# Norms with the variance per token on partitions, and grouped attention with its projections in three rounded passes

## The reference

```python
x = x + tanh(g_xattn[0]) * L0_xattn(layernorm(x), ctx)   # 16 heads of 16, causal
x = x + tanh(g_ffn[0])   * L0_ffn(layernorm(x))          # 8 experts, top 1, and a shared one
x = x + tanh(g_xattn[1]) * L1_xattn(layernorm(x), ctx)   # 16 latent heads over all 1444 keys
x = x + tanh(g_ffn[1])   * L1_ffn(layernorm(x))

def L1_ffn(hidden):                       # hidden: output of layer norm "n3"
    resid = hidden
    h = rmsnorm(hidden, ln1_w)            # "r0"
    q, k, v = h @ Wq, h @ Wk, h @ Wv      # 32 query heads, 4 key heads, of 128
    x = resid + causal_attention(rope(q), rope(k), v) @ Wo
    h = rmsnorm(x, ln2_w)                 # "r1"
    return x + experts(h) + shared(h)     # 32 experts, top 8
```

## Time and profile before

| | us |
|---|---|
| median of three runs | 1648.06 |
| profiled execution, whole | 1648.92 |
| its span | 1647.1 |
| TensorE, matmuls busy | 1497.2 (91%) |
| VectorE busy | 904.1 (55%) |
| GpSimd busy | 725.7 (44%) |
| ScalarE busy | 600.1 (36%) |
| granted TensorE clock, mean of the span | 0.927 of full |

### The profile page before, as it was taken

One profiled execution on the slowest core, in us unless ns is written; L12 is line 12 of the kernel. 1 busy time (PEld: TensorE's weight loads), 2 busy tenths in 40 slices (PEclk: granted clock), 3 DMA queues, 4 the chain that ended last, 5 costly groups with the idle time before them and its releaser, 6 DMA issues. The chain is left out here.

```text
span 1647.1 us, 19563 instructions
## 1 busy us (share of the span) xinstructions
PE 1497.2 (91%) x6852; PEld 1047.1 (64%) x6852; DVE 904.1 (55%) x1530; ACT 600.1 (36%) x1034; POOL 725.7 (44%) x541
## 2 busy tenths in 40 slices
PE   6897999799978999999999998589999997699998
PEld 3685466444435675766766765246666664699997
DVE  2563111335666767767776643656666664354444
ACT  2332121123331344334343343355555553243333
POOL 1750202026554877787787564034444441133332
PEclk8797999579987999999999999799999999799999
DMA  8004111430001010010110000300000001244331
GB/s 291 1 1 140 49 46 36 142 110 22 23 3 65 24 55 26 30 55 1 55 55 1 18 2 9 122 1 26 24 28 26 1 1 39 85 128 123 117 118 48
DMA packets 60311, 88.53 MB, mean 54 GB/s; under 512 B 7556, under 2 KB 44612, under 8 KB 60230
## 3 DMA queue, kind: packets, MB, share of 16 engines
q1 hardware_dynamic: 59206, 85.82, 16.3%
q0 software_dynamic: 1024, 1.64, 0.4%
HBM read 81.92 MB, written 5.41 MB: 53 GB/s over the span
## 5 line engine op out<-in xcount | busy, mean ns | idle before, releaser
L670 POOL TENSOR_TENSOR xc<-xc,prob 121x800 f32<-121x800 f32 x112 | 230.2, 2055 | 69.2 <-ACT prob L906 60.9
L906 ACT ACTIVATE prob<-PS 121x800 f32<-121x800 f32 x192 | 159.1, 837 | 266.6 <-PE PS L1802 266.6
L1248 DVE TENSOR_REDUCE mx<-PS 128x1 f32<-128x482 f32 (+1 forms) x312 | 185.3, 643 | 72.8 <-PE PS L1782 72.0
L594 POOL TENSOR_TENSOR e_wl<-e_wf,e_wh 128x768 fp32r<-128x768 f32 x33 | 70.8, 2146 | 185.9 <-ACT e_wh L830 160.0
L1817 PE MATMUL PS<-prob,kvn 121*64 121x400 f32 (+1 forms) x768 | 142.1, 521 | 0.9 <-ACT prob L906 0.9
L1799 PE MATMUL PS<-qs,kth 128*121 128x400 f32 (+1 forms) x384 | 116.1, 385 | 21.2 <-DMA qm<-nml 18.3
L1781 PE MATMUL PS<-kth,qs 128*128 128x482 f32 (+1 forms) x312 | 125.8, 403 | 8.3 <-DVE kl L1241 5.8
L691 POOL TENSOR_TENSOR q<-q,qt 128x400 f32<-128x400 f32 x64 | 66.0, 1031 | 143.2 <-DVE qt L1366 143.2
L1782 PE MATMUL PS<-kl,qm 66*128 66x482 f32 (+1 forms) x312 | 121.4, 389 | 0.0
L1802 PE MATMUL PS<-qm,kl 66*121 66x400 f32 (+1 forms) x384 | 108.2, 365 | 0.0
L1799 PEld LDWEIGHTS PS<-qs,kth 128*121 128x121 f32 (+1 forms) x384 | 68.4, 196 | 60.7 <-DMA qm<-nml 20.9
(11 more groups left out here) (256 smaller groups left out, 3202.4 us busy)
## 6 DMA issues: line engine op xcount, KB each, us to landing
e_wb<-routing SPq DMA_DIRECT2D x32, 400.0 KB, 4.0
wgu<-in_L_ffn_gate_up_proj SPq DMA_DIRECT2D x8, 1024.0 KB, 14.2
krt<-in_ctx_T SPq DMA_DIRECT2D x8, 722.0 KB, 4.1
ksw<-in_ctx_Tswap SPq DMA_DIRECT2D x8, 722.0 KB, 5.7
wdn<-in_L_ffn_down_proj SPq DMA_DIRECT2D x8, 512.0 KB, 8.8
wq<-in_L_ffn_Wq SPq DMA_DIRECT2D x4, 1024.0 KB, 6.5
wo<-in_L_ffn_Wo SPq DMA_DIRECT2D x4, 1024.0 KB, 7.5
e_wf<-in_L_ffn_Wg SPq DMA_DIRECT2D x32, 128.0 KB, 2.2
```

The costliest lines, as they stand in the source:

```text
L670: pool.tensor_tensor(accp, accp, prob[:, n % RING], ALU.add).then_inc(xb["ap"], 1)
L906: act.activation(prob[0:k, n % RING], PS[0:k, 2 * (n % 2):2 * (n % 2) + 2, 0:GC], ACT.Exp).then_inc(xb["ex"], 1)
L1248: dve.tensor_reduce(mx3[:, m, g:g + 1], PS[:, 4 + k % 3, 0:SEG[g][1]], AX.X, ALU.max).then_inc(xb["free"], 1)
```

## The change

1. **Norms.** The squares are now the stationary operand and one column of `mean_w` the moving one, so that the variance comes out with tokens on partitions, as 100 x 8 numbers. Root and reciprocal work on these (`nsd`, `nrs`), and eight matmuls against the identity (`spread`) bring the result back onto 128 partitions in PSUM, where the products read it. A root of a constant (`warm`) stands first on ScalarE. r0 takes its variance from that of n3 (`nms`: variance times the squared inverse root) and follows in the same stage; n3's output goes straight to `R`.
2. **Latent attention.** `accp` gets a second buffer; the merge of the accumulators, the sums and the projection come later in a batch (steps 5, 6, 14 and 3, 4 after the twelfth), the four reciprocals of one half in one block at step 8, of the other at steps 20 to 23. `UNITS` ends one step earlier, and the turned maxima stand ahead of the values block of step 20.
3. **Grouped attention.** Query and output projections run in three passes over rounded parts. ScalarE rounds the weights in pieces of 256 columns, GpSimd subtracts for the low parts, VectorE splits the inputs and each unit's result (`low_values2`). Weights are single buffered, queries lie in a ring of ten, outputs start at step 9 (`BACK`).
4. **End.** The residual is added ahead of the experts of block 1, in the routing stage, so that the last chain has one instruction a piece in place of two.

```diff
-        UNITS = (0, 0, 0, 0, 2, 4, 6, 8, 11, 14, 16, 18, 21, 24, 26, 29, 30, 32, 34, 36, 39, 39, 39, 39, 39)
+        UNITS = (0, 0, 0, 0, 2, 4, 6, 8, 11, 14, 16, 18, 21, 24, 27, 30, 31, 33, 36, 39, 39, 39, 39, 39, 39)
-        U2, LEAD = 2 * B * G2, 6
+        U2, LEAD, BACK = 2 * B * G2, 6, 9
...
+            def low_query_weights(m):
+                v = slice(m % HG * P, (m % HG + 1) * P)
+                pool.wait_ge(fs["wqh"], XQ + m + 1)
+                pool.tensor_tensor(wql[:, :, v], wq2[:, :, v], wqh[:, :, v].bitcast(fp32), ALU.subtract).then_inc(fs["wql"], 1)
...
+                act.activation(wqh[:, :, v], wq2[:, :, v], ACT.Copy).then_inc(fs["wqh"], 1)
...
+                if query_split(s) is not None:
+                    high_query_weights(query_split(s))
+                if output_split(s) is not None:
+                    high_output_weights(output_split(s))
...
+            def low_values2(v):
+                x, k, b = unit2(v)
+                y = 2 * x + k
+                dve.wait_ge(at["pve"], U0 + v + 1)
+                dve.tensor_tensor(o2l[:, y % 3, :, b % HB, :], PS[:, 3, 0:4 * S].rearrange("p (h s) -> p h s", s=S),
+                                  o2h[:, y % 3, :, b % HB, :].bitcast(fp32), ALU.subtract).then_inc(fs["ol"], 1)
...
                 pe.wait_ge(at["pte"], U0 + v + 1)
                 if v >= 1:
-                    pe.wait_ge(at["pve"], U0 + v)
+                    pe.wait_ge(fs["ol"], XQ + v)
...
-                    last_ = mm(PS[:, query_bank(n), 0:HALF], wq2[:, g % 2, c, (n % HG) * P:(n % HG + 1) * P], h1[:, c, half(n // HG % 2)],
+                    mm(PS[:, query_bank(n), 0:HALF], wqh[:, c, v], h1h[:, c, half(h)], start=(c == 0), stop=False)
+                    mm(PS[:, query_bank(n), 0:HALF], wqh[:, c, v], h1l[:, c, half(h)], start=False, stop=False)
+                    last_ = mm(PS[:, query_bank(n), 0:HALF], wql[:, c, v], h1h[:, c, half(h)], start=False, stop=(c == NC - 1))
...
+            def spread(t):
+                r, w, bank = 2 * ROOTS.index(t), int(t == "r0"), 6 if t == "r0" else 4
+                for h in range(2):
+                    pe.wait_ge(ns["rs"], r + h + 1)
+                    for i in range(HB):
+                        b = h * HB + i
+                        last = mm(PS[:, bank + h, i * S:(i + 1) * S], nrs[:, w, b:b + 1].to_broadcast([S, P]), ident[0:S, 0:S],
+                                  start=True, stop=True)
...
                 for h in range(2):
-                    pe.wait_ge(s["sq"], n + h + 1)
-                    for c in range(NC):
-                        last = mm(PS[:, 2 + h, 0:HALF], mean_w[:], sq[:, c, half(h)], start=(c == 0), stop=(c == NC - 1))
-                    last.then_inc(s["var"], 1)
+                    pe.wait_ge(ns["sq"], n + h + 1)
+                    for i in range(HB):
+                        for c in range(NC):
+                            last = mm(PS[0:S, 2 + h, i:i + 1], sq[:, c, toks(h * HB + i)], mean_w[:, 0:1],
+                                      start=(c == 0), stop=(c == NC - 1))
+                    last.then_inc(ns["var"], 1)
+                spread(t)
...
-                    if s in (0, 1) and b >= 1:
+                    if s in (0, 5) and b >= 1:
                         add_probabilities(2 * b - 1, s)
-                    if s in (KT, KT + 1):
+                    if s in (KT, KT + 3) and b < B:
                         add_probabilities(2 * b, s - KT)
...
-                    dve.tensor_tensor(R[:, c, half(h)], R[:, c, half(h)], PS[:, 4 + n, 0:HALF], ALU.add).then_inc(fin, 1)
-                    dve.wait_ge(fin, n + 1)
-                    dve.scalar_tensor_tensor(xT[:, c, half(h)], R[:, c, half(h)], gates[:, 3:4], xT[:, c, half(h)],
+                    dve.scalar_tensor_tensor(xT[:, c, half(h)], PS[:, 4 + n, 0:HALF], gates[:, 3:4], xT[:, c, half(h)],
```

More of the change, by code:

```diff
@@ L705, in _ @@
                     add_queries(s + LEAD)
+                if query_split(s - 1) is not None:
+                    low_query_weights(query_split(s - 1))
+                if output_split(s - 1) is not None:
+                    low_output_weights(output_split(s - 1))
             end_stage(pool, ST_F)
@@ L734, in norm @@
                         inp = src
[L735 to L738 removed]
+                    act.activation(sq[:, :, half(h)], inp[:, :, half(h)], ACT.Square).then_inc(ns["sq"], 1)
+                roots(t, None)
             norm("n0", None)
@@ L1024, in _, with centre, inverse_roots @@
         def _(dve):
+            def centre(t, src):
+                for h in range(2):
+                    dve.wait_ge(ns["mean"], 2 * ROOTS.index(t) + h + 1)
+                    dve.tensor_tensor(xc[:, :, half(h)], src[:, :, half(h)],
+                                      PS[:, h, None, 0:HALF].to_broadcast([P, NC, HALF]), ALU.subtract).then_inc(ns["xc"], 1)
+            def inverse_roots(t):
+                r, w = 2 * ROOTS.index(t), int(t == "r0")
+                for h in range(2):
+                    dve.wait_ge(ns["sd"], r + h + 1)
+                    dve.reciprocal(nrs[:, w, h * HB:(h + 1) * HB], nsd[:, w, h * HB:(h + 1) * HB]).then_inc(ns["rs"], 1)
@@ new lines, in scale @@
+            def scale(t, src, dst, w=None):
+                r, bank = 2 * ROOTS.index(t), 6 if t == "r0" else 4
+                for h in range(2):
+                    dve.wait_ge(ns["bc"], r + h + 1)
+                    if w is None:
+                        last = dve.tensor_tensor(dst[:, :, half(h)], src[:, :, half(h)],
+                                                 PS[:, bank + h, None, 0:HALF].to_broadcast([P, NC, HALF]), ALU.mult)
+                        if t == "n3":
+                            last.then_inc(ns["ms"], 1)
+                    else:
+                        if t == "r0":
+                            dve.wait_ge(ns["ms"], 3 + h)
+                        for c in range(NC):
+                            dve.scalar_tensor_tensor(dst[:, c, half(h)], src[:, c, half(h)], ln_w[:, w, c:c + 1],
+                                                     PS[:, bank + h, 0:HALF], ALU.mult, ALU.mult)
```

284 lines of the change are left out of this document (172 added, 112 removed).

## The result

The changed kernel takes 1601.82 us in the median of four runs (1592.79 to 1608.13), the kernel before 1648.76. The ratio is 0.970, 95% interval 0.965 to 0.976: 3% faster. I had said 1570, with a range of 1552 to 1592. So the direction was right and the size was wrong: 78 us were forecast and 47 came.

A forecast was written before the change was run, and what follows sets the result against it. TensorE, busy in 91% of the span, bounds it: matmul time in the attentions, chains in norms and batch changes. 1648.9 - 26 (grouped attention) - 26 (long attention) - 24 (norms) - 2 (tail) = 1570.9, said 1570; range 1552 to 1592.

The forecast's parts named there:

- None passes 4.07: Grouped attention: VectorE, ScalarE and GpSimd each have less work a step than TensorE's 4.07 us, save ScalarE's worst case, 4.1.
- I leave the loop at 3.80: Grouped attention, steps without output matmuls: the new VectorE subtraction leaves the two-engine loop at 3.80 us a step.
- fall by 0.27 each: Grouped attention, last steps: the six steps without queries save 0.27 us each, -1.6; the drain -0.4.
- The start of the stage: Grouped attention: weight roundings and low parts ahead of the first rotated query cost +2.5 us, between 0 and +6.
- The change of batch: Long attention, seven changes: waits for DMA and maxima go, -17.8 us, and half-clock loss, -17; together -35.
- The wait ahead of the sums: Long attention: the later merge on VectorE makes TensorE wait 0.3 to 0.7 us, fifteen times, +7 us.
- the values block and three banks (some 7 us of matmuls) cover it: Long attention: TensorE matmuls hide VectorE's 5 us block of four reciprocals, product and add.
- My rival of the shared port: Grouped attention: GpSimd's low parts hold VectorE's rotation, loop 4.52 us in 35 steps, +16, kernel 1586 us; chance 0.13.
- The terms by norm: Five norms, n3 counted with r0: -13 us for that pair, -1, -4, -3.5 and -2.5 for the others; sum -24.
- the choice of the full clock: Norms: n3 with r0 gives -14 us at full clock, -11 at half, -13 taken; other norms about -4 or -1.
- Norms at half clock: Norms: one-column matmuls leave TensorE nearly idle and the clock falls; norms give -13 us, kernel 1581 us; chance 0.18.
- End, -2.2 forecast: Tail: four adds of 0.56 us leave the last chain, -2.2; their replacements in the routing stage, uncovered, would cost +2.4.

The follow-up runs named there:

- all together: The changed kernel with low output weights a step earlier, low values first in last steps, adds under the projection, first-norm tables reordered, bf16 squares: 1564.97 us, ratio 0.948.
- the subtraction first: The changed kernel with the low part of the values made ahead of the maximum and its subtraction in every grouped-attention step: 1620.97 us, ratio 0.983.

## Why the prediction missed

**Grouped attention, -26 forecast, -4.1 measured: the largest error, 22 us.** The arithmetic of a step was right: 4.12 for 4.07 (2.4 us over 49 steps), and no other engine's sum of work is the bound. The step that failed is "None passes 4.07" together with "I leave the loop at 3.80". I had compared each engine's sum of work with the period, and had not asked when in a step each low part is ready. Three pieces:
- The low parts of the output weights come one step late, 9.8 us (shown). The weights are single buffered, so they cannot be made much earlier than just in time. The prediction has no word on this wait.
- The last steps: I had let them fall by 0.27 each. A loop through the subtraction holds them at 3.98, 6.0 us with the drain (shown); with the wait of 0.8 for `wol` in the first of them, they cost 7 more than forecast.
- The first nine steps take 37.8 us for 33.2 forecast. TensorE waits for `o2l` there too: 2.8 us at step 4, partly at half clock, and 0.7 a step from step 5 on, which holds these steps at 3.98 where "I leave the loop at 3.80" stands. That is read from the trace. No run isolates it: in three executions whose edits don't touch step 4 (low output weights earlier, reciprocals spread, all together) the wait there is 1.1 us, the nine steps take 35.9 and the stage's start some 1 us more. With the subtraction first they take 36.3, inside this scatter. So 2.7 to 5.2 us belong here, and what sets the 2.8 stays open.
The start of the stage, +2.5 forecast, measured +2.6.

**Long attention, -26 forecast, -17.7 measured.** The change of batch gave 29.9 and not 35. I had taken all of the time at half clock as half lost, though in part of it TensorE waited or ran at ScalarE's pace (my reading; no run tests it). The wait ahead of the sums was sized too large: a step with two units and the sums takes 2.88 and 2.72 us (steps 6 and 16), and took 2.62 before, 0.4 a batch, 2.5 in seven; forecast +7. The step that failed is "the values block and three banks (some 7 us of matmuls) cover it", by which the block of reciprocals cost nothing. With the product and the add behind it the block takes 7.1 us and not 5, since these two run beside GpSimd, and TensorE waits for the maxima: step 10 takes 2.8 us in the mean where such a step takes 1.6. My rival of the shared port was placed in the grouped attention, where the full steps stayed at 4.12. Here it costs 9.4 us (shown).

**Norms, -24 forecast, -15.6 measured.** The terms by norm were -1, -4, -3.5, -13, -2.5; measured +1.4, -2.6, -2.1, -11.9, -0.4. The step that failed is the choice of the full clock. The prices were right: a half's variance takes 1.3 to 1.4 us at full clock (n1) and 2.5 at half (n0), as the earlier trace rows had it. But I booked most norms near the full clock, and two thirds of their time ran at half: the granted clock is 0.52 to 0.77, in the n3 stretch 0.68. Before it was 0.71 to 0.87, and I had put it at "between 0.78 and 0.97". The rival "Norms at half clock" was nearer (-13). Its reason, that one-column matmuls make the clock fall, isn't shown: with the squares in bf16, whose variance takes 0.5 to 0.7 us a half, the clock of n3 with r0 is 0.68 as well. In the first norm I had counted one table load in the chain and there are two, since the load of Tanh, which began at 0.8 us before, now starts behind the wait for the gates; with another instruction ahead of that wait it starts at 0.8 again.

**End, -2.2 forecast, -2.3 measured.** The multiply-adds that replace the four adds cost nothing that can be seen.

The range was too narrow because its terms were treated as if each could only be mis-sized. The largest misses have one sign: they are waits that the change brings in and that a sum of busy times can't contain. The one that went the other way, the sums (2.5 for 7), helped to hide this in the total.

## What to carry to other kernels

- When a change adds an intermediate result, follow it through the queues: which step makes it, what stands ahead of it on that engine, which step needs it. An engine that is 60% busy can be late in every eighth step.
- An order that takes a wait away on one engine moves a deadline on another. The same change of batch was worth -30 us with VectorE's blocks moved out of its way and +48 without.
- Put long VectorE work where TensorE has its longest blocks; spreading it evenly cost 24 us here.

## What the hardware showed beside

- The stretch from the first projection to norm n1 (attention 0 in it), which the change leaves alone, takes 101.7 to 115.3 us in thirteen profiled executions. The time at half clock from the start to norm n1 is 17 us in the fastest and 48 to 55 in the slowest five, but also 48 in the changed kernel, where the stretch takes 110.3. That and the slow batches (64 to 66 us for 60 to 61) are large enough for most of the spread of 15 us between runs of one kernel, so that a gain of 10 us that one stage shows could not be seen in the medians. That they are its cause isn't shown, since only one execution of each kernel was profiled.
- An instruction of VectorE with both inputs in SBUF took 0.92 to 4.76 us for the same 121 x 800 elements: at most 0.99 in the batches where GpSimd's adds were gone, 4.76 where three GpSimd instructions ran beside it without a pause.
